# Layer norm and context intake written into the stages of a two-layer cross-attention and FFN kernel

## The reference

```
x = x + xattn0(layernorm(x), ctx)     # 32 q heads, 8 kv heads of 128, RoPE, mask, softmax
x = x + ffn0(layernorm(x))            # /128; silu(gate)*up; trunc(clip(.*128)); down; trunc(clip(.*128))
x = x + xattn1(layernorm(x), ctx)     # keys and values from context and x; q and k RMS-normed
x = x + ffn1(x)                       # layer norm inside, dynamic int8-like rounding, gelu, two linears
```

## Time and profile before

| | |
|---|---|
| median of 3 runs | 1591.58 us |
| the profiled execution's own time | 1589.58 us |
| its span, first to last instruction | 1587.8 us |
| TensorE busy | 1494.7 us (94%) |
| VectorE, ACT, GpSimd busy | 957.3, 588.2, 569.6 us |
| mean granted TensorE clock | 0.975 |
| loads | 60.56 MB read, 39 GB/s over the span |

### The profile page before, as it was taken

The page is one execution under the profiler, slowest core; times in us unless marked ns, Lnnn a source line. Parts: engine busy times, 40 slices in busy tenths (PEclk is TensorE's granted clock), DMA queues, the critical chain, the costliest instruction groups (busy, mean ns, idle before and its releaser), DMA issues. The chain is left out here.

```text
span 1587.8 us, 28705 instructions
## 1 busy us (share of the span) xinstructions
PE 1494.7 (94%) x11536; PEld 1281.4 (81%) x11536; DVE 957.3 (60%) x1954; ACT 588.2 (37%) x1416; POOL 569.6 (36%) x468
## 2 busy tenths in 40 slices
PE   4999999999999978998679999999999999999986
PEld 3788888888888867886569888888999888889973
DVE  6666566665666665664846545565555546555587
ACT  3222132222222215442235444443544444344456
POOL 2544363443535304662223222231222223141248
PEclk8999999999999998999879999999999999999998
DMA  6111020111102002220211101010111101010201
GB/s 177 40 41 41 28 63 25 48 34 34 53 16 67 1 21 60 79 55 0 71 50 34 35 28 41 14 55 2 41 28 28 41 28 41 1 54 16 72 10 53
DMA packets 81229, 64.44 MB, mean 41 GB/s; under 512 B 7280, under 2 KB 66928, under 8 KB 81104
## 3 DMA queue, kind: packets, MB, share of 16 engines
q1 hardware_dynamic: 80240, 62.47, 13.6%
q10 hardware_dynamic: 864, 0.20, 0.1%
HBM read 60.56 MB, written 2.10 MB: 39 GB/s over the span
## 5 line engine op out<-in xcount | busy, mean ns | idle before, releaser
L142 POOL TENSOR_TENSOR att_w_lo<-att_w_raw,att_w_hi 128x512 fp32r<-128x512 f32 x160 | 202.8, 1293 | 174.4 <-ACT att_w_hi L137 174.4
L1294 POOL TENSOR_TENSOR att_probs<-att_probs,att_total 128x512 f32<-128x512 f32 x64 | 82.8, 1294 | 476.7 <-DVE att_total L1033 357.6
L70 PE MATMUL att_proj<-att_w_hi,kv_hi 128*128 128x256 f32 x768 | 223.5, 291 | 8.6 <-PEq L223 8.6
L70 PE MATMUL att_proj<-att_w_lo,kv_hi 128*128 128x256 f32 x768 | 218.7, 285 | 0.0
L70 PE MATMUL att_proj<-att_w_hi,kv_lo 128*128 128x256 f32 x768 | 218.6, 285 | 0.0
L70 PE MATMUL att_proj<-att_w_hi,att_o_hi 128*128 128x512 f32 x512 | 206.0, 402 | 6.0 <-issue 3.9
L70 PE MATMUL att_proj<-kv_hi,att_w_hi 128*128 128x512 f32 x512 | 207.2, 405 | 0.0
L70 PE MATMUL att_proj<-kv_lo,att_w_hi 128*128 128x512 f32 x512 | 201.9, 394 | 0.0
L70 PE MATMUL att_proj<-kv_hi,att_w_lo 128*128 128x512 f32 x512 | 201.4, 393 | 0.0
L70 PE MATMUL att_proj<-att_w_lo,att_o_hi 128*128 128x512 f32 x512 | 200.9, 392 | 0.0
L70 PE MATMUL att_proj<-att_w_hi,att_o_lo 128*128 128x512 f32 x512 | 200.8, 392 | 0.0
(11 more groups left out here) (152 smaller groups left out, 2945.1 us busy)
## 6 DMA issues: line engine op xcount, KB each, us to landing
att_w_raw<-in_wq SPq DMA_DIRECT2D x64, 256.0 KB, 2.9
att_w_raw<-in_wo SPq DMA_DIRECT2D x64, 256.0 KB, 2.7
ln_stage<-in_ctx_t SPq DMA_DIRECT2D x8, 512.0 KB, 5.0
att_w_raw<-in_wk SPq DMA_DIRECT2D x16, 256.0 KB, 3.0
att_w_raw<-in_wv SPq DMA_DIRECT2D x16, 256.0 KB, 3.2
ffn_w_raw<-in_gate_t SPq DMA_DIRECT2D x10, 256.0 KB, 2.9
ffn_w_raw<-in_up_t SPq DMA_DIRECT2D x10, 256.0 KB, 3.1
ffn_w_raw<-in_down_t SPq DMA_DIRECT2D x10, 256.0 KB, 3.0
```

The costliest lines, as they stand in the source:

```text
L70: ins = eng.matmul(out, a, b, start=(first and n == 0), stop=(last and n == 3 * len(terms) - 1))
L142: eng.tensor_tensor(self.lo[:, chunk], self.raw[:, n % RAW_SLOTS], raw(self.hi[:, chunk]), ALU.subtract)\
L1294: eng.tensor_tensor(probs[:, u % 2, 0:n], probs[:, u % 2, 0:n], total[:, u % 2, 0:n].unsqueeze(2).broadcast_to([P, n, KL]), ALU.mult)\
```

## The change

The three norm blocks and `load_inputs` go. A class `Intake` has one small method for each step of one row tile, and each stage calls them at chosen places of each engine's order. `scale_rows` makes mean and 1/sqrt for four tiles, so a stage can begin with its first half. `load_ctx` loads the context in four parts of 512 KB, 256 columns each; two into `st.spare` (which also serves as `turn_a`, `turn_b`, `squares`), two into a part of `q_cols`. One raw weight ring (`st.w_raw`) serves all stages, so that a stage's SP queue can end with the next stage's first loads.

```
+def scale_rows(eng, st, chain, stage, h):
+    some = slice(4 * h, 4 * h + 4)
+    eng.wait_ge(st.stats_done, NT * stage + 4 * h + 4)
+    for t in range(4 * h, 4 * h + 4):
+        ins = eng.bn_aggr(st.agg[:, t], st.stats[:, t])
...
+class Intake:
+    def normalise(self, eng, t):
+        st, ring = self.st, len(self.xn)
+        eng.wait_ge(st.rows_scaled, HALF * self.stage + t // 4 + 1)
+        need(eng, self.turned, t - ring + 1)
+        eng.tensor_scalar(self.xn[t % ring], st.x[:, t], st.agg[:, t, 0:1], st.rstd[:, t:t + 1],
+                          ALU.subtract, ALU.mult).then_inc(self.xn_done[t // 4], 1)
...
```

A kv or q job waits for the parts it reads, no longer for all: the kv jobs of group 0 for `ctx_split` and (second attention) `x_split` of their tile, q jobs of group 0 in the first attention for `x_split` of their half. The tail of the FFN (`out_bank(t)` is `banks[(t + 4) % 8]`; the second part is VectorE's for each out tile, and GpSimd has none in it any more):

```
-            clipped.need(eng, 0, CF * HALF)
             split.need(eng, 0, 3 * CF)
             for t in range(NT):
+                if t % (NT // HALF) == 0:
+                    clipped.need(eng, 0, CF * HALF - 1 + t // (NT // HALF))
-                        last = eng.matmul(banks[t][:], hid[:m, c, t * P:(t + 1) * P], down[:m, c, :],
+                        last = eng.matmul(out_bank(t)[:], hid[:m, c, t * P:(t + 1) * P], down[:m, c, :],
...
+                out_chain.step(floor_steps(out_chain, eng, 0, P, t % 2))
+                eng.tensor_tensor(val[:, t % 2], flo[:, t % 2], sign[:, t % 2], ALU.mult).then_inc(out_signed, 1)
+                eng.wait_ge(out_signed, t + 1)
+                eng.scalar_tensor_tensor(st.x[:, t], val[:, t % 2], QBITS - 1, st.x[:, t], ALU.min, ALU.add).then_inc(out_added, 1)
+                eng.wait_ge(out_added, t + 1)
+                eng.bn_stats(st.stats[:, t], st.x[:, t]).then_inc(st.stats_done, 1)
+                if t == 4:
+                    scale_rows(eng, st, rows_chain, 2, 0)
```

More of the change, by code:

```diff
@@ L143, in split_chunk @@
            .then_inc(self.split, 1)
[L145 to L198, removed]
@@ L205, with load_ctx @@
+def load_ctx(eng, st, stage, h):
+    for q in range(2):
+        part = slice(2 * q * P, 2 * (q + 1) * P)
+        eng.dma_start(stage[:, :, part], st.ctx_cols[:, :, h * BANK + 2 * q * P:h * BANK + 2 * (q + 1) * P])\
+           .then_inc(st.ctx_landed[2 * h + q], 16)
 RSQRT_SEED = float(0x5F3759DF)
@@ L219, in rsqrt @@
     return last
[L222 to L308, removed]
-                eng.activation(ctx_dest(st.kv_hi, k), ctx_src(k), ACT.Copy).then_inc(ctx_rounded, 1)
-            for t in range(NT):
-                round_columns(t)
-                if ctx_t is not None and t < KT:
-                    round_ctx(t)
-                if t == NT // 2:
-                    weights.round_first(eng)
-        @block.tensor
-        def _(eng):
-            for t in range(NT):
-                eng.wait_ge(xn_done, t + 1)
-                if t >= 4:
-                    eng.wait_ge(drained, t - 3)
-                for k in range(KT):
-                    last = eng.transpose(cols[t % 4][:, k * P:(k + 1) * P], xn[:, t % 2, k * P:(k + 1) * P],
-                                         st.ident[:])
-                last.then_inc(turned, 1)
@@ L554, in finish, with attention @@
            .then_inc(self.summed[int(n in self.LATE)], 1)
-def attention(nc, st, tag, rope, weights, mask=None, tail=None):
+def attention(nc, st, tag, rope, weights, source=None, following=None, tail=None):
     KL = S if rope else 2 * S
@@ L668, in attention @@
         chained = sem("dve_chained")
+        late_stage = q_cols[:, 2:4].rearrange("p u b g s -> p (u b g s)").rearrange("p (k n) -> p k n", k=KT)
+        intake = Intake(st, f"{tag}_in", 0 if rope else 2, [probs_t[:, 0], probs_t[:, 1]], att + sco, (0, 1, 2, 3, 0, 1, 0, 1),
+                        not rope, [st.spare, late_stage], 0 if rope else 1)
         block = ctx.enter_context(nc.Block())
@@ L741, in q_job @@
                 eng.wait_ge(w_split, weights.ready(g, chunk))
+                if rope and g == 0:
+                    eng.wait_ge(intake.x_split, 4 * h + 4)
                 room(eng, job)
@@ L761, in turn_keys @@
                 need(eng, sco_drained, SJ * key_unit(g, h))
+                if g == 0 and h == 0:
+                    eng.wait_ge(intake.x_split, 4)
                 for i in range(TKH):
@@ L1476, in load_next @@
                     weights.load(eng, i, c + 1, m)
+            load_ctx(eng, st, st.spare, 0)
+            following.load(eng, 3)
             with eng.Fori(0, WIDE - 1) as c:
@@ L1480, in _ @@
             load_next(WIDE - 1, REST)
+            split.need(eng, 0, 3 * CF)
+            for n in range(3):
+                following.load(eng, n)
         @block.scalar
@@ L1488, in body @@
                         weights.round_chunk(eng, i, c, 1, 1 - sub, m_next)
+                if isinstance(c, int) and c == 0:
+                    for t in range(4, NT):
+                        intake.round_x(eng, t)
                 for h in range(HALF):
@@ L1496, in body @@
                     eng.activation(sign[:m, h], val[:m, h], ACT.Sign).then_inc(measured.sem, 1)
-            eng.activation(act[:, 0, 0:1], st.ones[:, 0:1], ACT.Silu).then_inc(primed, 1)
+            weights.round_chunk(eng, 0, 0, 0, 0, P)
+            weights.round_chunk(eng, 1, 0, 0, 0, P)
+            for t in range(4):
+                intake.round_x(eng, t)
+            weights.round_chunk(eng, 2, 0, 0, 0, P)
+            eng.activation(mag[:, 0, 0:1], st.ones[:, 0:1], ACT.Silu).then_inc(primed, 1)
             eng.wait_ge(primed, 1)
@@ L1511, in _ @@
             signed.start(eng)
+            for t in range(4):
+                intake.normalise(eng, t)
+            split.need(eng, 0, 2)
+            weights.split_chunk(eng, 2, 0, 0, 0, P)
             def body(c, sub, m, m_next):
@@ L1532, in _ @@
             chain = Chain(eng, chained, STEPS)
+            rows_chain = Chain(eng, st.sem(f"{tag}_rows_chained"))
+            weights.split_chunk(eng, 0, 0, 0, 0, P)
+            weights.split_chunk(eng, 1, 0, 0, 0, P)
+            for t in range(4):
+                intake.lower_x(eng, t)
+            scale_rows(eng, st, rows_chain, 1, 1)
+            for t in range(4, NT):
+                intake.normalise(eng, t)
+            for t in range(4, NT):
+                intake.lower_x(eng, t)
             def body(c, sub, m, m_next):
@@ L1575, in _ @@
             pair_full.start(eng)
+            for t in range(4):
+                intake.turn(eng, t)
             def body(c, sub, m, m_next):
@@ L1579, in body @@
                 for h in range(HALF):
+                    if isinstance(c, int) and c == 0:
+                        for t in range(4, 8 * h):
+                            intake.turn(eng, t)
+                        eng.wait_ge(intake.x_split, 4 * h + 4)
                     pair_drained.need(eng, c, h + 1 - PAIRS)
```

384 lines of the change are left out of this document (295 added, 89 removed).

## The result

The changed kernel takes 1577.0 us (median of four, 1574.4 to 1580.5) against 1591.4 for the kernel before: ratio 0.9912, 95% interval 0.990 to 0.9925. It gains 14.4 us where 39.7 were forecast, and 1577 lies outside 1543 to 1563.

What follows compares the result with a forecast made beforehand. TensorE was taken to set the time, with gains where it waits: 12.0 + 4.6 + 6.8 + 2.3 + 14.0 = 39.7 us off 1591.58 gives 1551.9, said as 1552; own range 1546 to 1558, with rivals (1) to (3) 1543 to 1563.

Steps and rivals of the forecast that it cites:

- the price of xn on GpSimd: All openings: normalising one tile by a GpSimd tensor_scalar takes 0.69 us, bounds 0.50 and 1.29.
- First opening, 12.0: Kernel start to scores of unit 0: scores at 38.6 instead of 50.6, 12.0 us gained, bounds 7 and 15.
- Into the FFN, 4.6: First attention's end into the FFN: second half's first product at 608.1 for 612.79, 4.6 us gained, bounds 1 and 7.
- Gate/up to down and the last out tile: FFN: down starts without waiting for the last clip, 6.8 us gained; last out tile's tail shorter, 2.3 us gained.
- Second attention, 14.0: Second attention's block start to scores of unit 0: 35.1 us instead of 49.1, 14.0 gained, bounds 9 and 17.
- Between the openings, 0: Everything between the openings: same TensorE instructions in the same order, so no gain or loss.
- the last sign: Last listed sign that the forecast is wrong: the units between the openings get longer.
- (1): Rival, chance 0.15: GpSimd and VectorE hold each other up in the openings, 10.1 us less gain, 1562.
- (2): Rival, chance 0.12: the clock stays high or comes up during the turns, so the openings' slow stretches go, 1544.6.
- (3): Rival, chance 0.07: the clock falls again in gaps the intake makes inside stages, 2.6 us each, about 10, 1562.
- (4): Rival, chance 0.03: slower, about 1594; unoverlapped round trips of 3.1 us by 24 tiles, deciding from 3.0 per tile.
- (5): Rival, chance 0.03: a queued load or table holds each opening, only the FFN's 9.1 us remains, 1582.

Runs made afterwards that it cites:

- e0: Changed kernel plus thirteen GpSimd operations of different operand forms ahead of its first weight split; subtract-multiply took 1.92 us with two immediates, 2.00 with a column.
- e1: Changed kernel with the scale by rstd left out, so xn subtracts the mean and multiplies by an immediate 1.0; 1571.8 us, ratio 0.9882.
- e6: Changed kernel plus fourteen GpSimd tensor_scalar operations of different operation pairs; pairs of multiply and add took 0.62 to 0.77 us, the others 2.0.
- e7: Changed kernel with xn written as multiply-add (x times rstd plus a prepared shift), still on GpSimd; 1555.5 us, ratio 0.9773.
- e3: Kernel before with only the FFN's tail changed: down's wait split by halves, out banks turned by four, VectorE alone finishing out tiles; 1580.8 us, ratio 0.9938.
- e8: e5 with ScalarE's rounding of the second attention's context tiles 6 and 7 moved ahead of x tiles 6 and 7; 1551.2 us, ratio 0.9748.
- e10: e7 with the second attention's context tiles 6 and 7 rounded earlier, as in e8; 1552.0 us, ratio 0.9765.
- e5: Changed kernel with xn on VectorE, first weight and context splits on GpSimd, and statistics of tiles 4 and 5 later; 1554.8 us, ratio 0.9776.
- e11: e7 with SyncE's first load held back behind two GpSimd memsets, about 1.3 us; 1557.5 us.
- e12: e7 with SyncE's first load held back behind five GpSimd memsets, about 3.2 us; 1558.5 us.

## Why the prediction was wrong

**The failed step is the price of xn on GpSimd**, in the part on prices: a tensor_scalar with one column operand, "0.69, the same form on the same engine", bounded by 0.50 and 1.29. It took 2.06. The row was read by its operands, shapes and engine, and the two operations it computes, multiply and add, weren't looked at; xn is a subtract and a multiply (e0, e1, e6). Its upper bound was GpSimd's two-tensor row, as if one tensor in could not cost more than two. With the forecast's price put back (e7) the kernel takes 1555.5, 3.5 above the forecast and inside its range. That it comes so near is partly luck, as the terms below miss by up to 4.4 in both directions. Among the signs of being wrong named beforehand were a tensor_scalar of over 1 us on GpSimd and waits for xn of over 20 us in the openings; they came at 2.06 and 29.4.

**First opening, 12.0.** 0.9 in the changed kernel, 9.1 in e7: there the scores start at 41.47 for 38.6. The first q job starts 2.5 us late (24.17 for 21.7), as VectorE takes the context and then the statistics later than forecast, the last of the first four at 14.06 for 12.7; the hold-up of small operations in the scales (1.22 and 0.87 for two of 0.16) is about the 1.6 that I had allowed. But the job then runs at the full clock, 0.47 for its first product, where I had 2.0 us of low clock, and by the end of q (1,1) e7 is at 36.7, where the forecast was: two errors that cancel, which is luck. What is lost is lost behind it. Turns 6 and 7 wait 2.85 us for xn, which stands in GpSimd's queue behind the rotation of q (0,1) and two context low parts (36.26 to 38.76), and these turns run at a clock of 0.50.

**Into the FFN, 4.6.** 0.0 and 3.8. Here 8.3 us of xn took the place of the norm stage that went. In e7 the xn of 1.73 makes TensorE wait 0.58 ahead of the next turn.

**Gate/up to down and the last out tile, 6.8 and 2.3.** 6.9 and 2.3 between the profiles at the points that the prediction used: both right, and by e3 they need nothing else of the change.

**Second attention, 14.0.** 8.6 and 16.5: at the right price it was under-forecast by 2.5. The window of this stretch has a granted clock of 0.73 in the kernel before, 0.82 in the changed kernel and 0.88 in e7, where I had counted a slow stretch of 3 us; how much of the 2.5 that is wasn't measured.

**Between the openings, 0.** Wrong, as the last sign warned: 3.4 us given back in the second attention by the changed kernel, 4.4 in two places by e7. One cause is shown: GpSimd's late context tiles hold up VectorE's small operations on the path to the first probabilities. The first unit takes 16.98 us before, and again in e8 and e10, where the hold-up is taken away; with it, it takes 20.67 in the changed kernel, 20.65 in e5 (clock 0.91) and 19.13 in e7 (clock 1.00 behind the same idle 2.4). Of the 3.7 lost there the changed kernel wins back 1.9 in later units, for a reason I didn't look for, and it loses 1.6 behind the last scores, where e1, the same there, loses nothing. The other is seen, but not explained: the clock falls in gaps at the first attention's end that it had outlasted before, 3 us in e7, e11 and e12. I had reckoned lower_ctx 6 and 7 only against the unit's normalise, 8 us later, and not against VectorE.

**The rivals.** (1) The hold-up is real but small: 1.2 us in a chain of small operations here and there, and 1.0 in two of e7's xn. The rule of the Trainium skill (SBUF — State Buffer, on the shared port pair), that the loser waits for the other's whole instruction, fits the 1.26 and 0.16 of one operation with and without GpSimd's subtraction of 1.26 beside it; it doesn't make the 2.06, as the same pair of operations takes 2.00 with VectorE idle. (2) and (3) both came, in different places: the first q job of e7 at the full clock, its turns 6 and 7 at the low one. (4) One of its terms was near: in the changed kernel a tile goes round in 2.06 by GpSimd alone, and with it all of the second opening's gain was lost. (5) came close in size, 9.2 of 14.4, for another reason: only in the first opening did loads come later than forecast (first kv product at 10.2 for 8.0), and e7 gains 9.1 there with the same loads.

## What to carry to other kernels

Before work is moved to another engine, look for a row there with the same operations, not only the same shape and operands; on GpSimd write a normalisation as multiply-add with a prepared shift. If an opening gets shorter, read the first unit behind it too: what was moved out of the way lands beside its small operations. And an edit that failed in the time may be one operation away from its forecast: put the forecast's price into the kernel and time it.

## What the runs showed of the hardware

GpSimd's tensor_scalar of 128x512 f32 takes 0.62 to 0.77 us where both operations are multiply or add, and 1.92 to 2.07 where one is a subtract or the pair is max and min; a subtract alone 1.57, a two-tensor multiply with a broadcast column 1.04. VectorE does the subtract-multiply in 0.54. Beside VectorE's subtractions of two tensors the 0.77 of multiply-add became 1.73 (e7), and beside GpSimd's a VectorE operation of eight columns took 1.26 for 0.16.
TensorE's granted clock around gaps of 2.0 to 2.4 us isn't settled by the gap: the same instructions behind the same 2.05 us of idle were run at a mean clock of 0.87 in one execution and 1.00 in another, which makes 3 us in 1550. Behind the first scores of the second attention the clock was 0.91 in the changed kernel and 1.00 in e7, each with 2.4 us of idle.
